# Where four delayed feature tiles stand in each batch of a coattention stage

## The reference, cut to what matters

```python
Sim = (e @ w1)[:, :, None] + (ctx @ w2)[:, None, :] + einsum('bid,bjd->bij', e * w3, ctx) + b_sim[0]
A = softmax(Sim, axis=2)
hq_hat = einsum('bij,bjd->bid', A, ctx)
Batt = softmax(max(Sim, axis=2), axis=1)
hc_bar = einsum('bi,bid->bd', Batt, e)
feats = concatenate([e, hq_hat, e * hq_hat, e * hc_bar], axis=-1)
x = x + tanh(g_xattn[1]) * (feats @ W_qv + b_qv)
```

## Time and profile before

| | |
|---|---|
| Median of 3 runs | 808.38 us (806.57 to 809.07) |
| Profiled execution, its own time | 809.36 us |
| Its span, first to last instruction | 807.4 us |
| Busy: PE, DVE, ACT, POOL | 706.4, 473.1, 373.3, 286.0 us |
| Mean granted TensorE clock | 0.935 of full |
| Coattention stage in the trace | about 565.8 to 722.8 us |
| Batch 1, 2, 3 (start of the transposes) | 604.2, 638.6, 672.9 us |

### The profile page before, as it was taken

How to read it: one execution, slowest core, us unless ns; L and a number is a source line. 1 busy time by engine, 2 the same in 40 slices (tenths; PEclk the granted TensorE clock), 3 DMA queues, 4 the chain that set the end, 5 groups by cost and what they waited for, 6 DMA issues and landing times. The chain is left out here.

```text
span 807.4 us, 11568 instructions
## 1 busy us (share of the span) xinstructions
PE 706.4 (87%) x3970; PEld 454.7 (56%) x3970; DVE 473.1 (59%) x852; ACT 373.3 (46%) x660; POOL 286.0 (35%) x477
## 2 busy tenths in 40 slices
PE   3699969999999997869899999998489999966886
PEld 1377734444444443754678787776266766752454
DVE  3576667787778760653844343434346546457985
ACT  0166635888888887435432232342222130202565
POOL 2355623434434432283001010010122346247797
PEclk9699977999999999898999999999598998996999
DMA  6001000000000001910020000000200000000001
GB/s 192 13 30 30 13 8 1 1 2 1 2 1 1 2 1 55 392 37 1 0 105 1 1 1 0 0 1 0 65 1 0 1 1 1 1 0 0 27 32 46
DMA packets 14106, 21.49 MB, mean 27 GB/s; under 512 B 2160, under 2 KB 11504, under 8 KB 13296
## 3 DMA queue, kind: packets, MB, share of 16 engines
q1 hardware_dynamic: 13200, 20.34, 7.5%
q10 hardware_dynamic: 864, 0.59, 0.2%
HBM read 18.83 MB, written 2.10 MB: 26 GB/s over the span
## 5 line engine op out<-in xcount | busy, mean ns | idle before, releaser
L564 DVE TENSOR_REDUCE mx<-ps_f 128x2 f32<-128x1024 f32 x128 | 150.2, 1219 | 45.1 <-PE ps_f L496 45.1
L639 ACT ACTIVATE prob<-ps_s 128x512 f32<-128x512 f32 x256 | 141.1, 603 | 33.4 <-PE ps_s L515 31.3
L515 PE MATMUL ps_s<-q_stacks,k_stacks 64*128 64x512 f32 x256 | 104.3, 459 | 0.3 <-ACT prob L639 0.3
L528 PE MATMUL ps_o<-prob,vst 128*32 128x256 f32 (+1 forms) x896 | 79.1, 426 | 0.7 <-ACT prob L639 0.4
L515 PEld LDWEIGHTS ps_s<-q_stacks,k_stacks 64*128 64x128 f32 x256 | 43.8, 188 | 60.0 <-ACT prob L639 28.2
L496 PE MATMUL ps_f<-k_stacks,q_stacks 64*128 64x512 f32 x256 | 66.1, 461 | 6.8 <-DVE mx L564 5.3
L1020 ACT ACTIVATE qs<-ps_g 128x512 f32<-128x512 f32 x40 | 23.9, 598 | 89.3 <-PE ps_u L904 89.3
L1087 DVE SCALAR_TENSOR_TENSOR h<-ps_u,most,qs 128x512 f32<-128x512 f32 x32 | 24.0, 751 | 62.6 <-ACT qs L1020 62.6
L589 POOL TENSOR_TENSOR q_stacks<-minus,q_stacks 128x512 fp32r<-128x512 f32 x32 | 40.6, 1272 | 43.5 <-ACT minus L630 43.5
L172 POOL TENSOR_TENSOR norm_tmp_att<-st 128x4 f32<-128x4 f32 x4 | 1.0, 238 | 142.5 <-DVE st L1126 142.5
L1529 ACT ACTIVATE qs<-ps_SC,nmax 128x512 f32<-128x512 f32 x16 | 11.0, 687 | 77.0 <-DVE nmax L1417 76.9
(11 more groups left out here) (278 smaller groups left out, 1573.5 us busy)
## 6 DMA issues: line engine op xcount, KB each, us to landing
up<-in_up SPq DMA_DIRECT2D x10, 256.0 KB, 6.7
x<-in_x SPq DMA_DIRECT2D x4, 512.0 KB, 8.1
ctxT<-in_ctxT SPq DMA_DIRECT2D x16, 128.0 KB, 2.0
ks<-in_ctxTC SPq DMA_DIRECT2D x1, 2048.0 KB, 11.9
ks<-in_ctx SPq DMA_DIRECT2D x1, 2048.0 KB, 18.1
out<-x SPq DMA_DIRECT2D x16, 128.0 KB, 1.7
down<-in_down SPq DMA_DIRECT2D x1, 1280.0 KB, 5.6
ks<-in_wqv SPq DMA_DIRECT2D x1, 1024.0 KB, 20.1
```

The lines of the kernel that those rows point to most:

```text
L515: pe.matmul(ps_s[n % 3][:, :], ks[rows(h), 2 * s + pair, kt * P:(kt + 1) * P], qs[rows(h), 2 * s + pair, :], start=True, stop=True).then_i ...
L528: last = pe.matmul(ps_o[HPAD * j:HPAD * (j + 1), cols], vst[:, s % 2, kt, HPAD * j:HPAD * (j + 1)], prob[:, kt % 2, j, cols], start=(kt == 0),
L564: dve.tensor_reduce(mx[:, f % 2, qt, 2 * pair:2 * pair + 2], ps_f[n % 2][:, :, :], AX_X, ALU.max).then_inc(used, 1)
L639: act.activation(prob[:, kt % 2, j, :], ps_s[n % 3][:, :], ACT.Exp, scale=SCALE)\
```

## The change: what it does

Only the order of steps changes, on TensorE and in the matching places on DVE. No instruction is added or removed; DMAs, tiles and the lists of ACT and GpSimd stay. Of the delayed feature tiles, 0 used to stand ahead of the similarity tiles, 1 between `attended(0)` and `attended(1)`, 2 between `context(2)` and `context(3)`, and 3 ahead of `pooled`. Now 0 stands after similarity 1, 1 after similarity 2, and 2 and 3 after `context(3)`. `context_transposes(3)` moves from behind `pooled` to between features 2 and 3, `attended(3)` changes places with `context_transposes(0)`. The steps in the batches without features are reordered in the same way.

```diff
@@ TensorE, batch(b, v)
                 if before:
                     pe.wait_ge(eT_ready, 2 * b + 1)
+                similarity(b, 0)
+                similarity(b, 1)
                 feature(0)
-                for q in range(QT):
-                    similarity(b, q)
+                similarity(b, 2)
+                feature(1)
+                similarity(b, 3)
                 attended(b, 0)
-                feature(1)
                 attended(b, 1)
                 context(b, 0)
                 attended(b, 2)
                 context(b, 1)
+                attended(b, 3)
                 context_transposes(b, 0)
-                attended(b, 3)
                 context(b, 2)
                 context_transposes(b, 1)
-                feature(2)
                 context(b, 3)
                 context_transposes(b, 2)
+                feature(2)
+                context_transposes(b, 3)
                 feature(3)
                 pooled(b, v)
-                context_transposes(b, 3)
@@ VectorE, batch(b, v, before, last)
                 maximum(b, 0)
+                maximum(b, 1)
                 updated(0)
-                for q in range(1, QT):
-                    maximum(b, q)
+                maximum(b, 2)
+                updated(1)
+                maximum(b, 3)
                 sim_maxima(b)
                 sum_inverses(b)
-                updated(1)
                 context(b, 0)
                 context(b, 1)
                 batch_maximum(b)
                 context_transposed(b, v, 0)
                 context(b, 2)
                 context_transposed(b, v, 1)
-                updated(2)
                 context(b, 3)
                 context_transposed(b, v, 2)
+                context_transposed(b, v, 3)
+                updated(2)
                 updated(3)
                 if not last:
                     normalise(b + 1, 1 - v)
                 pooled_weights(b)
-                context_transposed(b, v, 3)
```

## The result

The changed kernel took 825.1 us (median of 4 runs, 823.5 to 828.1) against 808.7 us before (806.6 to 809.8): a ratio of 1.021, 95% interval 1.0174 to 1.0246. In a second measurement it was 825.7 against 808.5 us, 1.021 (1.0185 to 1.0235). The forecast was 823, slower.

What follows compares the result with a forecast made beforehand. PE's own list was taken to bound the coattention stage, so uncovered waits lengthen each batch. Terms -6.3 + 7.8 - 2.4 + 5.7 + 1.8 + 0.7 + 0.5 + 6.9 = +14.7 us on 808.4 gave 823, range 814 to 830.

Steps and rivals of the forecast that it cites:

- Heads: Transposes to similarity 0: nothing saved in batch 1; 4.4 us in batches 2 and 3, saving 2.6 and 3.7 us.
- Feature 0: After similarity 1 it covers nothing: +7.8 us over three batches; similarity's waits for ACT's exponentials go, -2.4 us.
- Feature 1: Between attended(0) and attended(1) PE waits for ACT's copy, a 2.33 us gap: +1.9 us a batch, +5.7 together.
- Feature 2 and `context_transposes(3)`: context(3) waits uncovered for DVE, +0.6 us a batch, +1.8; two transposes ahead of DVE's chain, 0.24 us, +0.7 for three batches.
- For batch 0 the total: In batch 0, context_transposes(3) waits for DVE's scaling, 0.65, plus its own 0.24, less 0.34 us: +0.5 us.
- The clock over similarity: Similarity 0 and 1 run at low clock after longer idle time: 2.3 us a batch, +6.9; bounds 0 and 3.1 each.
- (a): Clock falls a second time, in the new gap behind attended(0), adding 6.9 us: 830 us; chance 0.10.
- (c): DVE's chain, not PE, sets the batch, so only the earlier similarity 0 counts: 801 us; chance 0.03.
- (d): Features cost and give the same wherever they stand, PE's busy time being unchanged: 808 us; chance 0.04.
- (b): Low clock falls on idle time and GpSimd no longer holds sT in batch 1: +4.7 us, 813 us; chance 0.11.

## Why the prediction was right

The mechanism held: each wait that was named for batches 1 to 3 appeared, with the length that batch 0 had given. The sum was +14.7 us; the medians differ by 16.3 and 17.2, and the stage grew by 17.8 in the profile. Two of its parts came out by luck.

- **Heads.** Forecast 4.4 us for batches 2 and 3, measured 4.31 in both. In batch 1 the forecast saved nothing, measured 6.6 for 6.9. That GpSimd's passes set it is shown by holding them.
- **Feature 0.** For this move alone +7 was expected and +7.5 measured; the opposite edit gave 10 back where 8 was expected. Nearly all of it is the clock: the 7.8 us that the feature costs in the open is about what the shorter heads and the waits give back. One reading was off: of the 1.6 us in batch 3 that were called waits for the exponential, only 0.7 is such a wait (of similarity for ACT's L1529, once in the stage before); about 0.5 is the low clock that lasted until 681.9.
- **Feature 1.** The gap is 2.33 us in the batch shown, as forecast, and undoing the move gave 5 us back.
- **Feature 2 and `context_transposes(3)`.** 0.6 + 0.24 a batch reckoned, 0.91 in the trace, 3 us by medians alone. For batch 0 the total, +0.6 for +0.5, was luck. The step itself cost 1.2 us (a wait of 0.78, for the copy L1452, and the transposes), and `pooled` ran partly at the low clock; but similarity of batch 0, which the change does not touch, took 8.97 us for 9.81, because the clock was full 3.8 us after it began, and 5.5 us before the change.
- **The clock over similarity.** 2.3 us a batch was taken. Matmuls ran at 1.2 GHz for 3.9, 6.1 and 3.8 us behind the start of similarity 0 in batches 1 to 3 (full again at about 612.1, 653.0 and 690.6), half of which is 6.9, the forecast; in the second profile it is 6.4. That the middle of the bounds was met so well is luck, and the reason given, a longer idle time ahead of similarity, is not shown: in batches 1 and 2 the clock was low before that gap began. This is where the range was widest, and it is what varies: in the second profile of the changed kernel transposes to feature 0 of batch 2 took 1.6 us less than in the first.
- **What was missed.** The last four features stood in no term. PE waits 1.4 us for wx ahead of them, 1.2 before, and the low clock cost 2.8 and 1.6 us there in the two profiles of the changed kernel, none before. It is most of why the stage grew by 17.8 and not 14.7. It can't be laid to one edit: the run with feature 1 put back had none of it, the run with the end of the batch put back had, and so had the kernel before with the passes held (low from 709.5 to 713.0). Why the clock falls there in some profiles and not in others stays open.
- **The rivals.** (a) The clock stays full in the gap behind `attended(0)`. (c) and (d) fall with the run of feature 0 alone; (b) with the profile after, where sT of batch 1 took 3.75 us and similarity ran at half clock. The chances of the forecast, (a) and (b), which all mean slower, add up to 0.93, where 0.94 stands.

## What to carry to other kernels

When work off the chain is moved, price it by what it stood over: the start times of the same two steps with it and without it (here batch 0, which has none) gave the length of each new wait within 0.1 us. To put such work where it hides 0.7 us of waiting (similarity for ACT) is a poor reason to take it from where it hides 1.7. The clock does not follow from these start times and has to be read by itself: a low stretch behind an idle gap can cost more than the gap, so shortening the gap, or filling it with matmuls that nobody reads, can pay where moving work does not. It need not: with the gap already shortened to 0.6 us the filler made the head 1.7 us shorter and the kernel no faster.

## What was not expected of the hardware

- With one filling matmul (1.02 us in the trace) in a gap of 1.5 us the clock stayed at 2.4 GHz in the two batches of the profile in which it had fallen before, and adding it made the kernel 0.3% faster.
- The clock fell while PE was at work, on `pooled` or the transposes (598.4 and 642.8 in the changed kernel), and not only in idle time.
- A DVE operation with two inputs in SBUF (L1464, two of them) took 3.86 us for 0.87 beside GpSimd's passes. With GpSimd's smaller tiles GpSimd lost most (3.12 us for 1.86), and DVE 0.1 us on sT and about 0.4 on the four operations behind it.
